# Turning four or six key tiles of the larger query groups by VectorE and DMA instead of TensorE, in a transformer block on one Trainium2 core

## The chip, the core and the metric

The kernel runs on one core of a Trainium2 chip (trn2). The metric is the time of one execution on the device in microseconds (us), the median of several runs. TensorE (PE) multiplies matrices, and PEld is its weight load; VectorE (DVE), ScalarE (ACT) and GpSimd (POOL) work beside it, and SyncE (SP) issues DMAs, each of which is carried out by the core's 16 DMA engines. Each engine runs its own list of instructions in order and waits only on semaphores.

## What is computed

One block with attention and a routed feed-forward network, in float32, on 2048 tokens of 128 features. The attention part, which takes most of the time, has 16 heads of 64 and is causal:

```python
qkv = jnp.einsum('bse,ehd->bshd', x, w_qkv)
q, k, v = jnp.split(qkv, 3, axis=-1)
logits = jnp.einsum('bqhd,bkhd->bhqk', q, k) / jnp.sqrt(jnp.float32(q.shape[-1]))
logits = jnp.where(mask, logits, neg)                      # causal
probs = jax.nn.softmax(logits, axis=-1)
out = jnp.einsum('bshd,hde->bse', jnp.einsum('bhqk,bkhd->bqhd', probs, v), w_out)
```

Ahead of it stands a layer norm with a scale and a shift, behind it a gated residual, a second layer norm, and a feed-forward network in which each token goes through one of 8 experts.

## The kernel before

The heads are taken in 8 pairs (`PAIRS`), the queries in 8 groups of 256 (`GROUPS`). A group g of a pair sees 2g+2 tiles of 128 keys (`tiles_of`), 72 tiles for all groups of a pair. Per pair and group the work is this:

- score (L803): for each of four rows r (two halves of 128 queries for each of two heads), TensorE makes the scores in pieces of up to 512 keys, each in one bank of a ring of four in PSUM.
- top (L1172, L1175, L1179): VectorE copies each piece into `probs`, which has one buffer for even and one for odd groups, and takes the row's maximum.
- exp (L1021): ScalarE makes the exponentials of a row in place, with their sum.
- turn (L814): the second product needs keys on the partitions, so TensorE transposes the 4 blocks of 128x128 of a key tile into one of three PSUM banks (`TURN_BANKS`). The last tile of a group has only 2 blocks.
- take (L1029 on ScalarE, L1197 on VectorE): one of the two copies the bank to one of 16 slots of `pT` (`PT_SLOTS`).
- pv (L832): TensorE multiplies the slot with the values, two heads in two halves of the array, and adds to `ps_o`. The tiles are taken in order, so those of a group must all be done before those of the next.
- sum, put, get, norm, out, add: the inverse sums are turned on VectorE (L1188, L1190), sent through DRAM by SyncE (put: 4 DMAs of L606; get: 2 DMAs of L617, which wait for the put to land), multiplied in (L1214), and the output projection follows (L845).
- proj, hi, lo: queries, keys and values of the next pair (L782, L786, L1007, L1151, L1155), placed between.

Each engine's order is computed ahead of time by the class `Plan`, from assumed durations of every step (`took`), conditions (`ready`) and a rule of choice (`choose_pe`, `choose`); `PV_BATCH`, `SCORE_LEAD`, `SCORE_TILES`, `TAKE_ACT` and `TAKE_DVE` are its constants. SyncE's order (`transfers`) is sorted by the same assumed times; 20 DMAs of zeros to DRAM (blank, L635) are put in it too. After the last score SyncE loads the expert weights (L640, L641, L645), the last into the buffer of `probs`. Then come the sorting of the tokens and the experts.

## Time and profile before

| | us |
|---|---|
| median of 3 runs | 987.63 (987.43 to 989.5) |
| the profiled execution | 984.52 |
| its span, first to last instruction | 982.7 |
| TensorE busy | 952.1 (97%) |
| VectorE busy | 708.8 (72%) |
| ScalarE busy | 675.3 (69%) |
| GpSimd busy | 110.2 (11%) |
| all DMA queues, share of 16 engines | 11.7% |

The engines overlap, so their busy times don't add up. A name such as L814 is a line of the kernel, and `ps<-ident,probs` are the tiles that an instruction writes and reads. One float32 matmul instruction of L832, L782 or L845 stands as two records in the trace, one of L803 or L814 as one. The duration of a matmul record holds the way through the array, so that the price of one in a row is the time from start to start.

### The profile page before, as it was taken

How to read it: one execution, taken by the hardware profiler on the slowest of the kernel's cores; microseconds unless marked ns; L12 is line 12 of the kernel's file. 1: busy time of each engine (PE TensorE's matmuls, PEld its weight loads, DVE VectorE, ACT ScalarE, POOL GpSimd, SP SyncE). 2: the span in 40 equal slices, each digit the busy share in tenths (PEclk: the TensorE clock that was granted, in tenths of full speed). 3: DMA queues.
4: the chain of work that ended last, by engine and by line, in shares of the span. 5: the costliest groups of instructions: out<-in, count | busy, mean ns of one | idle time of the engine just before them, and what ended most of it. 6: DMA issues, size and time to landing. Idle time of an engine off the chain costs nothing.

```text
span 982.7 us, 19699 instructions
## 1 busy us (share of the span) xinstructions
PE 952.1 (97%) x6851; PEld 747.2 (76%) x6851; DVE 708.8 (72%) x2362; ACT 675.3 (69%) x1245; POOL 110.2 (11%) x125
## 2 busy tenths in 40 slices
PE   3999999999999999999999999999999999999797
PEld 2677777777777777777777777777777777878797
DVE  5788648875788658784887758774887578986554
ACT  2887667666777658675876768666776677764475
POOL 0200001000100010000100010000100010202144
PEclk9999999999999999999999999999999999999899
DMA  3001100120011100110011000210010000005220
GB/s 81 10 14 50 26 21 15 31 51 20 11 36 25 29 18 21 50 26 20 15 32 34 23 23 12 51 26 20 14 31 18 12 8 11 27 14 176 64 64 26
DMA packets 56002, 30.78 MB, mean 31 GB/s; under 512 B 12455, under 2 KB 53203, under 8 KB 55906
## 3 DMA queue, kind: packets, MB, share of 16 engines
q1 hardware_dynamic: 54658, 27.41, 10.5%
q0 software_dynamic: 1248, 2.13, 0.7%
q8 instruction: 55, 0.90, 0.4%
q14 instruction: 41, 0.34, 0.1%
HBM read 18.21 MB, written 11.77 MB: 31 GB/s over the span
## 4 chain that ended last, share of the span: by engine, by line
PE 95%; DVE 2%; ACT 1%; DMA 1%; SPq 0%; issue 0%; POOLq 0%; POOL 0%; DVEq 0%; ACTq 0%
PE ps L803 27%; PE ps L832 25%; PE ps L814 25%; PE ps L782 6%; PE ps L786 3%; PE ps L845 3%; PE ps L956 2%; PE ps L967 2%; PE ps L931 0%; DMA probs<-in_L_wmod_dram 0%; DVE accT L1108 0%; PE ps L885 0%; PE ps L928 0%; DVE stats L1091 0%; PE ps L947 0%
## 5 line engine op out<-in xcount | busy, mean ns | idle before, releaser
L1021 ACT ACTIVATE probs<-probs,neg_max 128x128 f32<-128x128 f32 (+15 forms) x256 | 308.9, 1209 | 98.1 <-DVE neg_max L1179 96.4
L803 PE MATMUL ps<-k_both,q_both 128*128 128x512 f32 (+2 forms) x1280 | 360.2, 397 | 2.0 <-DVE k_both L1155 1.3
L814 PE MATMUL ps<-ident,probs 128*128 128x128 f32 x2176 | 297.7, 273 | 0.2
L1029 ACT COPY pT<-ps 128x512 f32<-128x512 f32 (+1 forms) x428 | 227.2, 564 | 87.6 <-PE ps L814 81.3
L814 PEld LDWEIGHTS ps<-ident,probs 128*128 128x128 f32 x2176 | 255.1, 141 | 42.3 <-issue 10.1
L1172 DVE TENSOR_SCALAR_CACHE_REDUCE probs<-ps 128x512 f32<-128x512 f32 (+1 forms) x384 | 247.0, 665 | 10.8 <-PE ps L803 8.7
L832 PE MATMUL ps<-pT,v_sb 128*64 128x256 f32 (+1 forms) x2304 | 250.0, 370 | 0.0
L803 PEld LDWEIGHTS ps<-k_both,q_both 128*128 128x128 f32 x1280 | 207.8, 190 | 50.5 <-issue 29.0
L832 PEld LDWEIGHTS ps<-pT,v_sb 128*64 128x64 f32 x2304 | 157.4, 137 | 80.5 <-issue 9.2
L707 POOL CAST k_both<-k_both 64x1024 fp32r<-64x1024 f32 x64 | 66.4, 1038 | 751.0 <-DVE k_both L1155 749.0
L1175 DVE CUSTOM_DVE_ANT_0 probs<-ps,causal 128x256 f32<-128x256 f32 (+3 forms) x256 | 130.5, 510 | 2.1 <-PE ps L803 1.2
L1197 DVE COPY pT<-ps 128x512 f32<-128x512 f32 (+1 forms) x148 | 96.9, 660 | 41.9 <-PE ps L814 40.5
L1151 DVE SCALAR_TENSOR_TENSOR q_both<-ps,q_both 64x512 fp32r<-64x512 f32 x64 | 44.1, 688 | 88.0 <-ACT q_both L1007 87.0
L782 PE MATMUL ps<-hT,w_pair 128*128 128x512 f32 x128 | 63.4, 609 | 0.9 <-ACT hT L993 0.9
L1014 ACT COPY v_sb<-ps 128x512 f32<-128x512 f32 x32 | 18.8, 586 | 58.8 <-PE ps L786 58.4
L1214 DVE TENSOR_TENSOR oT<-ps,rinv_b 128x512 f32<-128x512 f32 (+1 forms) x33 | 22.3, 675 | 40.4 <-PE ps L832 40.2
L1021 ACT ACTIVATION_READ_ACCUMULATOR probs<-probs,neg_max 128x1 f32 x256 | 49.5, 193 | 0.0
L1179 DVE TENSOR_REDUCE neg_max<-row_max 128x1 f32<-128x1 f32 (+3 forms) x256 | 39.8, 155 | 9.0
L1155 DVE TENSOR_TENSOR k_both<-ps,k_both 64x512 fp32r<-64x512 f32 x64 | 44.0, 687 | 1.4 <-ACT k_both L1007 0.2
L786 PEld LDWEIGHTS ps<-w_pair,hT 128*128 128x128 f32 x256 | 33.2, 196 | 12.9 <-issue 12.1
L1007 ACT ACTIVATE q_both<-ps 64x512 fp32r<-64x512 f32 x64 | 37.8, 590 | 5.5 <-PE ps L782 4.6
L1007 ACT ACTIVATE k_both<-ps 64x512 fp32r<-64x512 f32 x64 | 37.8, 590 | 1.5 <-PE ps L782 0.5
(142 smaller groups left out, 569.8 us busy)
## 6 DMA issues: line engine op xcount, KB each, us to landing
x_sorted<-blank SPq DMA_DIRECT2D x19, 458.5 KB, 5.3
rinv_b<-spread_rows SPq DMA_DIRECT2D x128, 64.0 KB, 2.6
spread_rows<-rinv_rows SPq DMA_DIRECT2D x256, 0.5 KB
probs<-in_L_ffn_W_dram SPq DMA_DIRECT2D x1, 2048.0 KB, 11.1
w_pair<-in_L_attn_w_qkv_dram SPq DMA_DIRECT2D x24, 64.0 KB, 2.2
hT<-x_sorted SPq DMA_DIRECT2D x23, 65.5 KB, 1.8
x_sb<-in_L_attn_x_dram SPq DMA_DIRECT2D x4, 256.0 KB, 5.1
wo_pair<-in_L_attn_w_out_dram SPq DMA_DIRECT2D x8, 64.0 KB, 1.8
```

Of the source, the lines that this page charges most:

```text
L707: nc.gpsimd.tensor_copy(k_split[h][own_half(1 - h), :, cols], k_split[h][own_half(h), :, cols]).then_inc(k_doubled[c], 1)
L782: pe.matmul(ps_ring[:, s.bank, :], w_pair[:, p % 2, j, :], hT[:, c * BANK:(c + 1) * BANK], start=True, stop=True).then_inc(bank_full[s.ban ...
L786: m = pe.matmul(ps_ring[:, s.bank, P * t:P * t + P], hT[:, (TPC * c + t) * P:(TPC * c + t + 1) * P], w_pair[:, p % 2, 2, :], start=True, s ...
L803: m = pe.matmul(ps_ring[:, s.bank, 0:w], q_split[r % 2][:, q0:q0 + P], k_split[r % 2][:, part, k0:k0 + w], start=(part == 0), stop=(part = ...
L814: m = pe.transpose(ps_turn[:, n % TURN_BANKS, P * r:P * r + P], probs[:, g % 2, r, j * P:j * P + P], ident[:])
L832: m = pe.matmul(ps_o[D * h:D * h + D, o_half + P * u0:o_half + QG], v_sb[:, j, D * h:D * h + D], turned[:, u0:2, h, :], start=(j == 0), st ...
L1007: m = act.mul(dst[own_half(h), c * BANK:(c + 1) * BANK], ps_ring[own_half(h), bank, :], Q_SCALE if j == 0 else 1.0)
L1021: act.activation(row, row, ACT.Exp, bias=neg_max[:, g, r:r + 1], accum_out=row_sum[:, g, r:r + 1]).then_inc(exp_done, 1)
L1029: act.copy(pT[:, n % PT_SLOTS, lo:BANK], ps_turn[:, n % TURN_BANKS, lo:BANK]).then_inc(turn_taken[n % TURN_BANKS], 1)
L1172: dve.tensor_scalar(row, ps_ring[:, bank, 0:w], 1.0, LOWEST, ALU.mult, ALU.max, accum_out=highest).then_inc(bank_free[bank], 1)
L1175: dve.tensor_tensor_reduce(row, ps_ring[:, bank, 0:w], causal[:, BANK - w:], 1.0, LOWEST, ALU.add, ALU.max, highest).then_inc(bank_free[ba ...
L1197: dve.tensor_copy(pT[:, n % PT_SLOTS, lo:BANK], ps_turn[:, n % TURN_BANKS, lo:BANK]).then_inc(turn_taken[n % TURN_BANKS], 1)
```

## The change

For the groups 4 to 7 the first key tiles (4 of group 4, 6 of each of the groups 5, 6 and 7, together 22 of the 72 tiles of a pair) are no longer turned by TensorE. Instead:

- shuffle, VectorE: one instruction for each row r transposes the 32x32 blocks of these tiles from `probs` into `staged`. It waits for the row's exponentials, and the first of a group also for the previous group's DMAs to have landed (`moved`).
- move, SyncE: 16 DMAs a group, one for each pair of a source quarter a and a target quarter b of the partitions. Each takes 32 partitions by 4 or 6 tiles by 512 B from `staged` to `turned_far`, so that the blocks come to lie transposed as a whole. They wait for the group's four shuffles and for the previous group's products with `turned_far`.
- pv: the products of a group start with the tiles that TensorE turned and end with the moved ones, read from `turned_far`; the first of those waits for all 16 DMAs of the group.

`staged` and `turned_far` have one buffer each. To make room, `pT` goes from 16 to 8 slots, and the even buffer of `probs` is shortened. The first score pieces of the group after next now also wait for the shuffles that read the same buffer. The constants of the plan change, so that the order of all engines is another one.

```diff
-PT_SLOTS = 16
-PV_BATCH = 15
-SCORE_LEAD = 1.6
-SCORE_TILES = 24.0
-TAKE_ACT = -1500.0
-TAKE_DVE = 0.0
+PT_SLOTS = 8
+STAGED = 6
+FAR = {4: 4, 5: 6, 6: 6, 7: 6}
+ISSUE = 430.0
+LAND = 4000.0
+PV_BATCH = 8
+SCORE_LEAD = 1.4
+SCORE_TILES = 18.0
+TAKE_ACT = 0.0
+TAKE_DVE = 2500.0
...
+def pv_order(g):
+
+    return list(range(far(g), tiles_of(g))) + list(range(far(g)))
...
-        turns = [(p, g, j) for p, g in groups for j in range(tiles_of(g))]
+        turns = [(p, g, j) for p, g in groups for j in range(far(g), tiles_of(g))]
+        pvs = [(p, g, j) for p, g in groups for j in pv_order(g)]
+        self.moves = [(p, g) for p, g in groups if far(g)]
...
+    def move_at(self, m):
+
+        if m not in self.moved:
+            p, g = self.moves[m]
+            begin = max(self.at("shuffle", p, g, r) for r in range(4))
+            if m:
+                q, f = self.moves[m - 1]
+                begin = max(begin, self.at("pv", q, f, far(f) - 1), self.move_at(m - 1)[0] + 16 * ISSUE)
+            if begin >= NEVER:
+                return NEVER, NEVER
+            self.moved[m] = begin + HOP, begin + HOP + 16 * ISSUE + LAND
+        return self.moved[m]
...
+                if s.kind == "move":
+                    g, a = s.key[1], s.key[2]
+                    m = plan.move_no[p, g]
+                    sp.wait_ge(shuffled, 4 * m + 4)
+                    if m:
+
+                        q, f = plan.moves[m - 1]
+                        sp.wait_ge(pv_done, plan.order[q, f, far(f) - 1] + 1)
+                    for b in range(P // SQUARE):
+                        sp.dma_start(turned_far[b * SQUARE:(b + 1) * SQUARE, 0:far(g), a, :],
+                                     staged[a * SQUARE:(a + 1) * SQUARE, 0:far(g), b, :]).then_inc(moved, 16)
+                elif s.kind == "w1":
...
+                elif s.kind == "w2":
...
+                    if j < far(g):
+                        if j == 0:
+                            pe.wait_ge(moved, 256 * plan.move_no[p, g] + 256)
+                        of_head = turned_far[:, j, :, :].rearrange("p a (u h i) -> p h u a i", u=2, h=2)
...
+                    if past and far(past[1]) and c == 0:
+
+                        dve.wait_ge(shuffled, 4 * plan.move_no[past] + r + 1)
...
+                elif s.kind == "shuffle":
+
+                    r, m = s.key[2], plan.move_no[p, g]
+                    dve.wait_ge(exp_done, 4 * (p * GROUPS + g) + r + 1)
+                    if m and r == 0:
+                        dve.wait_ge(moved, 256 * m)
+                    dve.transpose(staged[:, 0:far(g), :, r * SQUARE:(r + 1) * SQUARE],
+                                  probs[g % 2][:, r, 0:far(g) * P].rearrange("p (j b i) -> p j b i", j=far(g), i=SQUARE)
+                                  ).then_inc(shuffled, 1)
```

The line numbers of the changed kernel differ; its steps keep their order in the text. L874 is its score, L885 its turn, L910 its pv, L923 its out, L667 its move, L686 its put, L697 its get, L715 its blank, L1254, L1257 and L1261 its top, L1269 its shuffle and L1288 its take on VectorE.

TensorE, fourth pair, the end of group 5's turns and its products. Before:

```order
L814 MATMUL ps<-ident,probs 128x128 x6
L832 MATMUL ps<-pT,v_sb 64x256 x2
L832 MATMUL ps<-pT,v_sb 64x128 x2
L832 MATMUL ps<-pT,v_sb 64x256 x22
L832 MATMUL ps<-pT,v_sb 64x128 x2
L803 MATMUL ps<-k_both,q_both 128x512 x2
L803 MATMUL ps<-k_both,q_both 128x384 x2
L803 MATMUL ps<-k_both,q_both 128x512 x2
L845 MATMUL ps<-oT,wo_pair 128x512
```

The same place in the changed kernel:

```order
L885 MATMUL ps<-ident,probs 128x128 x2
L874 MATMUL ps<-k_both,q_both 128x512 x2
L874 MATMUL ps<-k_both,q_both 128x384 x2
L874 MATMUL ps<-k_both,q_both 128x512 x2
L910 MATMUL ps<-pT,v_sb 64x256 x10
L910 MATMUL ps<-pT,v_sb 64x128 x2
L910 MATMUL ps<-turned_far,v_sb 64x256 x12
L885 MATMUL ps<-ident,probs 128x128 x4
L874 MATMUL ps<-k_both,q_both 128x512 x2
L885 MATMUL ps<-ident,probs 128x128 x4
L874 MATMUL ps<-k_both,q_both 128x512 x2
L923 MATMUL ps<-oT,wo_pair 128x512
```

Twelve of group 5's products now read `turned_far` and stand behind those of the tiles that TensorE turned, and the projection of the output moves behind them.

SyncE, fourth pair, groups 3 to 6. Before:

```order
L606 DMA spread_rows<-rinv_rows 4x32 x4
L617 DMA rinv_b<-spread_rows 64x2x128 x2
L606 DMA spread_rows<-rinv_rows 4x32 x4
L617 DMA rinv_b<-spread_rows 64x2x128 x2
L635 DMA x_sorted<-blank 128x7x131
L606 DMA spread_rows<-rinv_rows 4x32 x4
L617 DMA rinv_b<-spread_rows 64x2x128 x2
L635 DMA x_sorted<-blank 128x7x131
```

The changed kernel, groups 4 to 7 of the same pair and the start of the next:

```order
L686 DMA spread_rows<-rinv_rows 4x32 x4
L667 DMA turned_far<-staged 32x4x128 x8
L697 DMA rinv_b<-spread_rows 64x2x128 x2
L715 DMA x_sorted<-blank 128x7x131
L667 DMA turned_far<-staged 32x4x128 x8
L686 DMA spread_rows<-rinv_rows 4x32 x4
L697 DMA rinv_b<-spread_rows 64x2x128 x2
L715 DMA x_sorted<-blank 128x7x131
L667 DMA turned_far<-staged 32x6x128 x16
L686 DMA spread_rows<-rinv_rows 4x32 x4
L697 DMA rinv_b<-spread_rows 64x2x128 x2
L715 DMA x_sorted<-blank 128x7x131
```

After these rows come 16 moves of group 6, the put of group 7, and group 7's moves in pieces of 4, 8 and 4, with group 7's get and the next pair's first put between the pieces. In the last pair the load of the third weight tensor (L680) stands before the last 4 moves of group 6, and the other two (L672, L673) before all 16 of group 7.

VectorE, fourth pair, the end of group 5. Before:

```order
L1151 SCALAR_TENSOR_TENSOR q_both<-ps,q_both 64x512 x2
L1188 RECIPROCAL rinv<-row_sum 128x4
L1190 STREAM_TRANSPOSE rinv_rows<-rinv 128x32
L1197 COPY pT<-ps 128x512
L1172 TENSOR_SCALAR probs,row_max<-ps 128x512
L1197 COPY pT<-ps 128x256
L1172 TENSOR_SCALAR probs,row_max<-ps 128x384
```

The same place in the changed kernel:

```order
L1229 SCALAR_TENSOR_TENSOR q_both<-ps,q_both 64x512 x2
L1279 RECIPROCAL rinv<-row_sum 128x4
L1281 STREAM_TRANSPOSE rinv_rows<-rinv 128x32
L1269 STREAM_TRANSPOSE staged<-probs 128x24x32 x4
L1316 SCALAR_TENSOR_TENSOR accT<-ps,gate_a,accT 128x512
L1257 ISA probs,row_max<-ps,causal 128x256
```

The four shuffles of group 5 stand in one run behind its sums, and the copies of turned tiles have left this place.

## Rows read from the trace of the kernel before

**Rows 1.** page, parts 1 and 2: busy engines; granted clock

```profile
PE 952.1 (97%) x6851; PEld 747.2 (76%) x6851; DVE 708.8 (72%) x2362; ACT 675.3 (69%) x1245; POOL 110.2 (11%) x125
...
PEclk9999999999999999999999999999999999999899
```

**Rows 2.** busy us (records) by stretch: PE, PEld, DVE, ACT, POOL, clock, DMA

```profile
266.00:287.47 21.47, 21.47 (x137) 17.18 (x137) 19.39 (x66) 17.83 (x32) 2.08 (x2) 1.00 0.05 14
179.20:287.47 108.27, 108.24 (x779) 83.62 (x780) 79.71 (x254) 76.96 (x136) 8.30 (x8) 1.00 0.10 26
```

**Rows 3.** the chain that ended last: shares by line; two of its pieces

```profile
by line: PE ps L803 27.0%; PE ps L832 24.9%; PE ps L814 24.7%; PE ps L782 5.5%; PE ps L786 3.2%; PE ps L845 2.9%; PE ps L956 2.3%; PE ps L967 2.1%; PE ps L931 0.5%; DMA probs<-in_L_wmod_dram 0.5%; DVE accT L1108 0.4%; PE ps L885 0.4%; PE ps
...
179.20 4.04 PE ps L832 x40
...
287.47 4.04 PE ps L832 x40
```

**Rows 4.** timeline of TensorE: start, duration, instruction, records

```profile
436.34 0.72 PE L803 MATMUL ps<-k_both,q_both 128*128 128x512 f32 x2
436.89 0.60 PE L814 MATMUL ps<-ident,probs 128*128 128x128 f32 x4
437.25 0.71 PE L803 MATMUL ps<-k_both,q_both 128*128 128x512 f32 x2
```

**Rows 5.** groups by form: copies out of PSUM, block transposes

```profile
L1029 ACT COPY pT<-ps 128x512 f32<-128x512 f32 x379 | 210.5, 587 | 78.2 <-PE ps L814 72.1 <-PE ps L832 2.4
...
L1197 DVE COPY pT<-ps 128x512 f32<-128x512 f32 x133 | 90.6, 686 | 17.7 <-PE ps L814 16.3 <-DVE onehot L1276 0.2
...
L1190 DVE STREAM_TRANSPOSE rinv_rows<-rinv 128x32 f32<-128x32 f32 x64 | 13.5, 212 | 2.2
...
L1197 DVE COPY pT<-ps 128x256 f32<-128x256 f32 x15 | 6.4, 424 | 24.2 <-PE ps L814 24.2
```

**Rows 6.** timeline of VectorE: start to start of a copy

```profile
440.37 0.69 DVE L1197 COPY pT<-ps 128x512 f32<-128x512 f32 x1
440.97 0.68 DVE L1172 TENSOR_SCALAR_CACHE_REDUCE probs<-ps 128x512 f32<-128x512 f32 x1
```

**Rows 7.** timeline of SyncE: DMA issues

```profile
453.06 1.26 SPq L606 DMA_DIRECT2D spread_rows<-rinv_rows  x4
455.20 1.23 SPq L617 DMA_DIRECT2D rinv_b<-spread_rows  x2
456.48 1.62 SPq L579 DMA_DIRECT2D w_pair<-in_L_attn_w_qkv_dram  x3
```

**Rows 8.** the loads of x: ns of one issue, min, median, max

```profile
L586 SPq DMA_DIRECT2D x_sb<-in_L_attn_x_dram x4: 434/480/507, 0.8 to 3.4; - x4
```

**Rows 9.** page, part 6: KB each, median us to landing

```profile
x_sorted<-blank SPq DMA_DIRECT2D x19, 458.5 KB, 5.3
rinv_b<-spread_rows SPq DMA_DIRECT2D x128, 64.0 KB, 2.6
...
w_pair<-in_L_attn_w_qkv_dram SPq DMA_DIRECT2D x24, 64.0 KB, 2.2
```

**Rows 10.** the 5.3 us of one blank DMA; DMA share before last

```profile
398.80:404.10 5.30, 5.30 (x34) 3.95 (x31) 4.21 (x13) 2.30 (x4) 0.00 (x0) 1.00 0.43 113
```

**Rows 11.** the last score of a group 4 on TensorE

```profile
498.91 0.48 PE L803 MATMUL ps<-k_both,q_both 128*128 128x256 f32 x2
```

**Rows 12.** ScalarE's last exponential of that group

```profile
501.71 1.37 ACT L1021 ACTIVATE probs<-probs,neg_max 128x1280 f32<-128x1280 f32 x1
```

**Rows 13.** timeline of SyncE: the expert weights

```profile
893.84 0.78 SPq L640 DMA_DIRECT2D w_rows<-in_L_ffn_W_dram  x1
894.67 6.49 SPq L641 DMA_DIRECT2D experts<-in_L_ffn_b_dram  x1
901.20 1.90 SPq L645 DMA_DIRECT2D probs<-in_L_ffn_W_dram  x1
```

**Rows 14.** that stretch: DMA share

```profile
898.00:911.00 13.00, 12.86 (x113) 9.73 (x110) 6.03 (x25) 4.22 (x9) 4.33 (x5) 1.00 1.01 343
```

More of the change, by code:

```diff
@@ L53, in tiles_of, with far @@
     return 2 * g + 2
+def far(g):
+    return FAR.get(g, 0)
+def pv_order(g):
+    return list(range(far(g), tiles_of(g))) + list(range(far(g)))
 def chunks(g):
@@ L103, in __init__ @@
         ends = [(PAIRS - 1, i) for i in range(len(parts_of(PAIRS - 1)))]
-        keys = dict(score=scores, turn=turns, pv=turns, out=norms,
+        keys = dict(score=scores, turn=turns, pv=pvs, shuffle=shuffles, out=norms,
                     proj=[(p, c, j) for p, c in parts for j in range(3)], back=ends,
@@ L113, in __init__ @@
         self.number = {key: i for i, key in enumerate(turns)}
+        self.order = {key: i for i, key in enumerate(pvs)}
+        self.move_no = {key: i for i, key in enumerate(self.moves)}
         self.total = {kind: len(of) for kind, of in keys.items()}
@@ L119, in __init__ @@
         self.taken = {}
+        self.moved = {}
         self.mode = ""
@@ L144 @@
                  act=("hi", "value", "take", "exp", "mod2", "wtake"),
-                 dve=("norm", "sum", "lo", "add", "resid", "top", "take", "smalls", "fresh", "pick", "slots", "ends"))
+                 dve=("norm", "sum", "lo", "shuffle", "add", "resid", "top", "take", "smalls", "fresh", "pick", "slots", "ends"))
     FIRST = dict(act=("hi", "value"), dve=("sum", "norm", "lo"))
@@ L166, in ready @@
             free = 0.0
-            if key[2] == 0 and p + g and min(groups_of(*self.part_of(p, g))) == g:
+            if key[2] == pv_order(g)[0] and p + g and min(groups_of(*self.part_of(p, g))) == g:
                 free = at("norm", *self.part_of(*group_before(p, g)))
-            return max(at("take", *key), at("value", p, key[2] // 4), free)
+            return max(self.turned_at(key), at("value", p, key[2] // 4), free)
+        if kind == "shuffle":
+            m = self.move_no[p, g]
+            return max(at("exp", *key), self.move_at(m - 1)[1] if m else 0.0)
         if kind == "out":
@@ L183, in ready @@
             if past and k0 < tiles_of(past[1]) * P:
-                behind = at("turn", past[0], past[1], min((k0 + w) // P, tiles_of(past[1])) - 1)
+                behind = at("shuffle", past[0], past[1], key[2]) if far(past[1]) else 0.0
+                over = min((k0 + w) // P, tiles_of(past[1])) - 1
+                if over >= far(past[1]):
+                    behind = max(behind, at("turn", past[0], past[1], over))
             return max(at("score", *key), behind)
@@ L220, in get_from, with turned_at @@
         return max(self.at("sum", p, g) + PUT, free)
+    def move_at(self, m):
[9 more added lines that the diff above has]
+        return self.moved[m]
+    def turned_at(self, key):
+        p, g, j = key
+        return self.move_at(self.move_no[p, g])[1] if j < far(g) else self.at("take", *key)
     def part_of(self, p, g):
@@ L241, in transfers @@
         self.blanks = [(i, min(i + BLANK_ROWS, rows // P)) for i in range(0, rows // P, BLANK_ROWS)]
+        for m, (p, g) in enumerate(self.moves):
+            for a in range(4):
+                steps.append((self.move_at(m)[0] + 4 * ISSUE * a, "move", (p, g, a)))
+        p, g = PAIRS - 1, GROUPS - 1
+        steps.append((self.at("score", p, g, 3, chunks(g) - 1), "w1", (p,)))
+        steps.append((max(self.at("turn", p, g - 1, tiles_of(g - 1) - 1),
+                          self.at("shuffle", p, g - 1, 3) if far(g - 1) else 0.0) + HOP, "w2", (p,)))
         quiet = [(p, g) for p in range(PAIRS - 1) for g in range(GROUPS - 4, GROUPS - 1)]
@@ L276, in took @@
                         "rank": 700.0, "total": 400.0}[kind] + switch
+        if kind == "shuffle":
+            return far(key[1]) * P / 0.96 + 100.0
         if kind == "top":
@@ L331, in choose_pe @@
         score_at = place("score", lambda k: (k[2] * chunks(k[1]) + k[3]) / (4.0 * chunks(k[1])))
-        turn_at = place("turn", lambda k: k[2] / float(tiles_of(k[1])))
+        turn_at = place("turn", lambda k: (k[2] - far(k[1])) / float(tiles_of(k[1]) - far(k[1])))
         waiting = 0
         for key in self.ahead["pv"]:
-            if self.at("take", *key) > now:
+            if self.turned_at(key) > now:
                 break
@@ L1026, in _ @@
                     if n >= PT_SLOTS:
-                        act.wait_ge(pv_done, n - PT_SLOTS + 1)
+                        act.wait_ge(pv_done, plan.order[plan.turns[n - PT_SLOTS]] + 1)
                     lo = 0 if j <= 2 * g else QG
@@ L1194, in _ @@
                     if n >= PT_SLOTS:
-                        dve.wait_ge(pv_done, n - PT_SLOTS + 1)
+                        dve.wait_ge(pv_done, plan.order[plan.turns[n - PT_SLOTS]] + 1)
                     lo = 0 if j <= 2 * g else QG
```

66 lines of the change are left out of this document (39 added, 27 removed).

## Prediction

> **What bounds the kernel now.** First the page's busy shares and its clock row: TensorE is busy for 952.1 of 982.7 us, at full granted clock in nearly every slice [rows 1]. Then stretches: one pair in the middle, 179.20 to 287.47, takes 108.27 us, and TensorE is busy for 108.24 of them, VectorE for 79.71, ScalarE for 76.96 [rows 2]; the product of each pair's group 4 starts 108.27 us after that of the pair before [rows 3]. So in the eight pairs nothing but TensorE's own list sets the time. Then the chain by line: the scores (L803) hold 27.0%, the products (L832) 24.9%, the turns (L814) 24.7% [rows 3]. What leaves TensorE there shortens the kernel, as long as nothing else becomes late.
>
> **TensorE's gain.** The turns' share is 24.7% of 982.7 = 242.7 us [rows 3]. A pair has 64 key tiles of 4 blocks and 8 last ones of 2, the 8 pairs 2176 blocks: 0.1115 us each. The change removes 22 of 72 tiles of a pair, 4 blocks each: 88 blocks, 9.81 us a pair, 704 blocks and **78.5 us** in all. In the same way one record of L832 costs 0.106 us (72 x 8 tiles of 4 records), so a tile of products 0.42; a query or key projection of 512 columns 0.84 (L782, 128 records), an output projection 0.86 (L845, 66 records). A score piece of 512 keys and a turned tile together take 0.91 us (436.34 to 437.25) [rows 4], so the piece is 0.46; I take 0.35 and 0.24 for pieces of 384 and 256.
>
> **VectorE and ScalarE.** By the order of the two kernels VectorE loses 82 copies of 512 columns and 8 of 256, 59.6 us by their durations; ScalarE loses 94 of 512 and gains 8 small ones, some 52 us [rows 5]. VectorE gains 96 shuffles of 768 elements a partition and 32 of 512. Such a size isn't in the trace. The nearest rows are the 32-element block transpose, 212 ns, and the copies from PSUM, 424 ns for 256 and 686 for 512 columns, so 1.02 ns a column behind a start of 162 [rows 5]. One column per 1.02 ns gives 195 for 32 columns, two steps per column 227; 212 lies between. Start to start a 512 copy takes 0.60 us [rows 6]. I take one step per column, 0.88 us for a shuffle of 768 and 0.62 for 512; the other end is 1.7 and 1.15. The sum for VectorE is 96 x 0.88 + 32 x 0.62 = 104 us against 60 removed: about 5.5 us more a pair, 85 of some 100. The Trainium skill (Vector Engine (DVE) Microarchitecture Reference, section 3.8) says that the transposing front end sustains one element per cycle and lane; by that my value stands, but no row here has a long one.
>
> **The path of the moved tiles.** The turn was on TensorE's own list; the moved tiles come by VectorE, SyncE and the DMA engines, and TensorE stands still if they are late, since nothing of its list can pass the waiting product. Price of one move on SyncE: the nearest in form is the load of x, rows of 512 B in four runs, 0.434 to 0.507 us, median 0.480 [rows 8]. In a row, puts take 1.26/4 = 0.32, loads of w_pair 1.62/3 = 0.54, gets 1.23/2 = 0.62 [rows 7]. I take 0.50 for one move, with ends 0.32 and 0.62 by issue alone. Data: a blank DMA, 128 x 7 = 896 packets of 524 B, filled 0.43 of 5.3 us on 16 engines [rows 10], 0.041 us per packet and engine. A move of six tiles is 192 packets, 12 per engine, 0.49 us: just within the issue. Landing: 2.2 to 2.6 us after the start of an issue for 64 KB [rows 9]; I take 2.2.
>
> From the landing of one group's tiles to that of the next: four shuffles 3.6 us (the first waits for that landing), 15 x 0.50 = 7.5 to the last issue, 2.2 to its landing, in all **13.3 us**. The group's put and get (1.3 + 0.9 wait + 1.2, and a blank 0.6) run beside the shuffles for groups 5 and 6. Against it stands what TensorE has to do between two groups' first moved products, by the order of the changed kernel at the prices above:
> - group 4 to 5: 12 pieces of 512, 2 of 384, 4 of 256, 22 blocks, 8 and a half tiles of products, one out: 14.5 us. No stall, 1.2 to spare.
> - 5 to 6: 10 and 1 pieces, 30 blocks, 12 and a half tiles of products, out and proj: 15.7. No stall, 2.4 to spare.
> - 6 to 7: 2, 2 and 4 pieces, 44 blocks, 14 and a half tiles: 14.1. Here SyncE also does group 7's get and the next pair's first put (1.2 + 1.3) between the moves: 15.8. **Stall 1.7.**
> - group 4 has no group ahead of it. From its last score to its last exponential the trace shows 499.2 to 503.1, 3.9 us [rows 11, 12]; then sum, one shuffle and put 1.7, 8 moves 4.0, get and blank 1.8, 7 moves 3.5, landing 2.2: 17.1. TensorE has 16.7 in between: **stall 0.4.**
>
> So 2.1 us a pair. Next is density. In the last stretch of a pair, 21.47 us, VectorE is busy for 19.39 already [rows 2]. Some 22 blocks leave it there, 2.5 us; VectorE gains group 7's four shuffles, 3.5, and loses about three copies of 0.6: 21.1 of work against 19.0 of TensorE's. The scores run up to 1.4 groups ahead and take part of it up; I count half, **1.0 a pair** (0 to 3). With only 8 slots the products come in more batches, 74 runs against 68, at some 0.15 each: 0.9 us in all.
>
> **The end of the last pair.** There SyncE's weight loads come ahead of moves. Before, they fill the DMA engines completely for 13 us at 343 GB/s (share 1.01) [rows 14], and the second issue held SyncE for 6.49 us, so that it came free 7.3 us after the first [rows 13]. In the changed order all 16 moves of group 7 stand behind these two: 7.3 + put 1.3 + 4 moves 2.0 + get 1.2 + 11 moves 5.5 + 2.2 = 19.5 from the last score, where TensorE has 15.4: 4.1 us. Group 6's last four stand behind a load of 2.1 MB (6.1 us at that rate), of which the 2.4 to spare are covered: 3.7. Together **7.8 us** (0 to 16).
>
> **Sum.** 78.5 - 8 x 3.1 - 0.9 - 7.8 = 45.0. The profiled execution took 984.52 us, 1.8 more than its span; 939.5 is what I expect of it. The median of the runs is 3.1 above the profiled one, so the forecast is **942.6 us**.
>
> **Rivals.**
> 1. The moves are fully hidden. An issue of 0.45 (the shortest load of x and a gap of 0.02) takes 0.75 off each path: group 4 is free, group 7 stalls 0.95, and if VectorE's dense stretch is taken up and the end costs 3, 67 us are saved: 921. For it: the DMA engines are only 10% busy [rows 2]; against it: VectorE is close to full.
> 2. The gain is mostly eaten, but not lost. An issue of 0.62, as the gets take: 1.8 us more per path, stalls 2.2 + 0.6 + 0 + 3.5 = 6.3, with density 7.3 a pair: 8 x 2.5 - 8.7 = 11 us saved, 976.
> 3. **Slower**: the moves are bound by data, since each reads 32 partitions and writes 32. From 0.65 us a move the stalls of a pair (3 x 2.28 + 0.9 = 7.7, with density and the end's share 9.8) equal the gain; at twice the packet time, 0.98 for six tiles and 0.65 for four, they are 2.7 + 6.0 + 4.8 + 8.9 = 22.4 a pair, and the kernel would take about 1105. No row has a DMA on so few partitions with so many packets, so neither end is excluded. The Trainium skill (SBUF — State Buffer, section on the DMA port swizzle) says that DMA bandwidth depends on how many of 16 SBUF ports the partitions reach, and by its table 32 neighbouring ones reach 8; by that rule the packets take up to twice as long and this case is the one, by the issue rows it isn't unless those packets lose more than a third.
> 4. Slower: shuffles take two steps per column, 1.7 us. The paths grow by 3.3 (group 4: 0.6): stalls 1.0 + 2.1 + 0.9 + 5.0 = 9.0, density 4: 13 a pair against 9.8, so 1022. For it: the 212 ns row; against it: it is as near to the other value.
> 5. The products with `turned_far` read runs of 32 columns. If that cost them double, 176 tiles x 0.42 = 75 us are lost, and the time doesn't change. No row shows such a read.
>
> **How the numbers follow.** Forecast (928 to 965) 0.52; rival 1 0.16; rival 2 (965 to 985.6) 0.13; no change within 0.2%, about what a measurement can tell, 0.04, with rival 5 in it; rival 3 0.10; rival 4 0.05. So faster 0.81, same 0.04, slower 0.15. Below 915 I leave 0.03 and above 985 the slower cases, so the range is 915 to 985.
>
> **What would show it.** TensorE: 1472 blocks of turns at the same 0.11 us; idle time in front of the first product with `turned_far`, put down to a DMA, 0 to 2 us, most in group 7, and longer at the end of the last pair. VectorE: shuffles of 0.9 to 1.0 us; 1.7 means rival 4. SyncE: 512 issues of 0.45 to 0.55; DMA share near 1 while they run and a landing far over 2.6 us after the last issue mean rival 3. Products with `turned_far` over 0.106 us a record mean rival 5. The forecast is wrong if VectorE, which waits for landed tiles in front of the next tops, holds up scores, so that TensorE waits for banks more than for moves.

## The result

The changed kernel takes 1032.53 us (median of 4 runs, 1032.12 to 1034.67) where the kernel before takes 988.08 beside it: a ratio of 1.045, with a 95% interval of 1.043 to 1.047. It is slower by 4.5%, where I had forecast a gain of 4.6%. The profiled execution of the changed kernel spans 1030.6 us, 47.9 more than the profiled one before. That one took 984.52 us, 3.6 less than the 988.08 here, so some 3.6 of the 47.9 are a difference between executions of the same kernel.

First the page of the changed kernel, its busy engines, its clock row and its chain by line (to be held against [rows 1] and [rows 3]).

```profile
span 1030.6 us, 18821 instructions
...
PE 919.4 (89%) x6147; PEld 681.8 (66%) x6147; DVE 758.8 (74%) x2400; ACT 626.7 (61%) x1159; POOL 110.2 (11%) x125
```

```profile
by line: SPq L667 24.1%; PE ps L910 11.5%; DMA turned_far<-staged 7.2%; PE ps L874 6.4%; PE ps L885 6.4%; issue 5.9%; DVE staged L1269 5.5%; PE ps L853 4.1%; DVE probs L1254 3.9%; PE ps L857 2.8%; PE ps L1034 2.3%; PE ps L1045 2.0%; DVE pro
```

TensorE did get its 704 blocks less, but its busy time fell by 33 us only, and it now stands idle for 111.2 us where it did for 30.6. In the chain, the largest single line is no longer one of TensorE's: SyncE's issue of the moves (L667) holds 24.1%.

Next the waits for the moves, of TensorE (PE), and the wait of VectorE (DVE) for the products that stand behind them (us in total, times, longest), and the moves' own row (duration of one issue in ns: min, median, max).

```profile
DVE oT L1305 <- PE ps L910: 63.1, 16, 8.7
...
PE ps L910 <- DMA turned_far<-staged: 58.7, 26, 11.1
```

```profile
L667 SPq DMA_DIRECT2D turned_far<-staged x512: 585/611/1881, 73.1 to 948.9; - x171
```

The fourth pair shows the path from landing to landing. First SyncE and then TensorE: start, duration, instruction, records, and in brackets the idle time ahead of it.

```profile
428.63 0.60 SPq L715 DMA_DIRECT2D x_sorted<-blank  x1
429.98 10.68 SPq L667 DMA_DIRECT2D turned_far<-staged  x16
441.22 1.26 SPq L686 DMA_DIRECT2D spread_rows<-rinv_rows  x4
...
445.98 10.60 SPq L667 DMA_DIRECT2D turned_far<-staged  x16
...
462.21 3.33 SPq L667 DMA_DIRECT2D turned_far<-staged  x4
465.64 1.27 SPq L697 DMA_DIRECT2D rinv_b<-spread_rows  x2
467.01 5.26 SPq L667 DMA_DIRECT2D turned_far<-staged  x8
472.32 1.51 SPq L686 DMA_DIRECT2D spread_rows<-rinv_rows  x4
473.93 2.56 SPq L667 DMA_DIRECT2D turned_far<-staged  x4
```

```profile
422.72 2.60 PE L910 MATMUL ps<-pT,v_sb 128*64 128x256 f32 x24 [1.26 <-DVE oT L1305]
426.43 1.95 PE L910 MATMUL ps<-turned_far,v_sb 128*64 128x256 f32 x16 [1.11 <-DMA turned_far<-staged]
...
442.43 2.81 PE L910 MATMUL ps<-turned_far,v_sb 128*64 128x256 f32 x24 [0.16 <-DMA turned_far<-staged]
...
458.63 2.76 PE L910 MATMUL ps<-turned_far,v_sb 128*64 128x256 f32 x24
...
478.27 4.38 PE L910 MATMUL ps<-turned_far,v_sb 128*64 128x256 f32 x24 [4.52 <-DMA turned_far<-staged]
```

```profile
426.39 3.56 DVE L1269 STREAM_TRANSPOSE staged<-probs 128x768 f32<-128x768 f32 x4 [1.84 <-DMA turned_far<-staged]
```

```profile
440.05 2.25 DMA turned_far<-staged
```

The last row is of the chain: from the start of the last issue to the landing. So the path is 3.56 for four shuffles, 10.07 from 429.98 to the last issue at 440.05, and 2.25 to land: from 426.39 to the next product of moved tiles at 442.43 it is 16.0 us, where I had 13.3. Of the 2.7 that are missing, 15 x 0.165 = 2.5 are the price of an issue. In front of group 7, with a get and a put between the moves, it is 19.6 (458.63 to 478.27), and TensorE is idle for 4.52 of them.

The stall has a second price. Below are stretches of that place: us, busy time of each engine, then the granted clock, the DMA engines' share and GB/s.

```profile
473.80:478.30 4.50, 0.03 (x2) 0.06 (x3) 1.02 (x5) 1.18 (x3) 0.00 (x0) 0.97 0.41 96
478.30:480.00 1.70, 1.70 (x9) 1.05 (x10) 0.00 (x0) 0.00 (x0) 0.00 (x0) 0.50 0.21 62
480.00:483.00 3.00, 3.00 (x21) 1.94 (x18) 0.32 (x1) 0.00 (x0) 0.00 (x0) 0.75 0.09 27
483.00:486.00 3.00, 3.00 (x18) 2.04 (x17) 0.52 (x2) 1.92 (x4) 0.00 (x0) 1.00 0.38 91
```

After 4.5 us without work TensorE was granted 0.50, its 1.2 GHz level, at once, and 0.75 on average over the 3 us behind; it was at 2.4 GHz again only after 483. The mean granted clock of the whole run is 0.965, before 0.993. The products with moved tiles, which stand right behind the stalls, carry most of it.

```profile
L910 PE MATMUL ps<-turned_far,v_sb 128*64 128x256 f32 x704 | 104.1, 454 | 58.7 <-DMA turned_far<-staged 58.7
```

A whole pair, from one group 7's moved products to the next pair's, now looks like this; before, it was 108.27 us with 108.24 busy [rows 2].

```profile
478.27:590.27 112.00, 102.62 (x689) 74.85 (x689) 85.53 (x256) 71.09 (x126) 8.29 (x8) 0.99 0.33 77
```

Of its 9.4 us of idle time the brackets below hold 8.7, and 7.5 of these are for moves.

```profile
532.57 2.60 PE L910 MATMUL ps<-pT,v_sb 128*64 128x256 f32 x24 [1.25 <-DVE oT L1305]
537.36 1.95 PE L910 MATMUL ps<-turned_far,v_sb 128*64 128x256 f32 x16 [2.19 <-DMA turned_far<-staged]
...
553.79 2.81 PE L910 MATMUL ps<-turned_far,v_sb 128*64 128x256 f32 x24 [0.59 <-DMA turned_far<-staged]
570.55 2.81 PE L910 MATMUL ps<-turned_far,v_sb 128*64 128x256 f32 x24 [0.41 <-DMA turned_far<-staged]
590.27 2.37 PE L910 MATMUL ps<-turned_far,v_sb 128*64 128x256 f32 x11 [4.28 <-DMA turned_far<-staged]
```

### The profile page after: what moved, and what is told of

Same layout as the page of the kernel before. It is cut to its first block, busy times and chain, and to the rows that moved or that the text cites. A ratio compares the mean times of both kernels' runs of the same rounds, so it can differ in the third digit from the quotient of the medians.

```text
span 1030.6 us, 18821 instructions
## 1 busy us (share of the span) xinstructions
PE 919.4 (89%) x6147; PEld 681.8 (66%) x6147; DVE 758.8 (74%) x2400; ACT 626.7 (61%) x1159; POOL 110.2 (11%) x125
## 4 chain that ended last, share of the span: by engine, by line
PE 38%; SPq 27%; DVE 17%; DMA 8%; issue 6%; ACT 3%; another core or an unknown queue 1%; POOLq 0%; POOL 0%; DVEq 0%; ACTq 0%
SPq L667 24%; PE ps L910 11%; DMA turned_far<-staged 7%; PE ps L874 6%; PE ps L885 6%; DVE staged L1269 6%; PE ps L853 4%; DVE probs L1254 4%; PE ps L857 3%; PE ps L1034 2%; PE ps L1045 2%; DVE probs L1257 2%; SPq L686 1%; SPq L697 1%; ACT probs L1099 1%
## 5 line engine op out<-in xcount | busy, mean ns | idle before, releaser
L1099 ACT ACTIVATE probs<-probs,neg_max 128x128 f32<-128x128 f32 (+15 forms) x256 | 308.9, 1207 | 150.2 <-DVE neg_max L1261 147.3
L874 PE MATMUL ps<-k_both,q_both 128*128 128x512 f32 (+2 forms) x1280 | 358.8, 397 | 9.0 <-DVE probs L1254 2.8
L1254 DVE TENSOR_SCALAR_CACHE_REDUCE probs<-ps 128x512 f32<-128x512 f32 (+1 forms) x384 | 245.5, 666 | 22.5 <-PE ps L885 10.8
L874 PEld LDWEIGHTS ps<-k_both,q_both 128*128 128x128 f32 x1280 | 203.7, 189 | 78.7 <-issue 28.7
L1107 ACT COPY pT<-ps 128x512 f32<-128x512 f32 (+1 forms) x342 | 178.1, 549 | 113.5 <-PE ps L885 104.8
L885 PE MATMUL ps<-ident,probs 128*128 128x128 f32 x1472 | 213.1, 274 | 1.4 <-ACT probs L1099 0.5
L885 PEld LDWEIGHTS ps<-ident,probs 128*128 128x128 f32 x1472 | 174.8, 141 | 42.3 <-issue 15.4
L910 PE MATMUL ps<-pT,v_sb 128*64 128x256 f32 (+1 forms) x1600 | 174.3, 366 | 9.9 <-DVE oT L1305 7.5
L910 PE MATMUL ps<-turned_far,v_sb 128*64 128x256 f32 x704 | 104.1, 454 | 58.7 <-DMA turned_far<-staged 58.7
L910 PEld LDWEIGHTS ps<-pT,v_sb 128*64 128x64 f32 x1600 | 108.2, 137 | 72.8 <-issue 12.4
L1257 DVE CUSTOM_DVE_ANT_0 probs<-ps,causal 128x256 f32<-128x256 f32 (+3 forms) x256 | 130.6, 510 | 26.4 <-PE ps L874 26.1
L1269 DVE STREAM_TRANSPOSE staged<-probs 128x768 f32<-128x768 f32 (+1 forms) x128 | 108.7, 886 | 41.9 <-DMA turned_far<-staged 40.5
L910 PEld LDWEIGHTS ps<-turned_far,v_sb 128*64 128x64 f32 x704 | 66.0, 163 | 88.2 <-issue 74.9
L1099 ACT ACTIVATION_READ_ACCUMULATOR probs<-probs,neg_max 128x1 f32 x256 | 49.0, 191 | 0.0
L1288 DVE COPY pT<-ps 128x512 f32<-128x512 f32 (+1 forms) x58 | 37.4, 656 | 12.2 <-PE ps L885 10.4
L1261 DVE TENSOR_REDUCE neg_max<-row_max 128x1 f32<-128x1 f32 (+3 forms) x256 | 39.8, 156 | 8.9
## 6 DMA issues: line engine op xcount, KB each, us to landing
x_sorted<-blank SPq DMA_DIRECT2D x19, 458.5 KB, 5.2
```

The costliest lines, as they stand in the source:

```text
L874: m = pe.matmul(ps_ring[:, s.bank, 0:w], q_split[r % 2][:, q0:q0 + P], k_split[r % 2][:, part, k0:k0 + w], start=(part == 0), stop=(part = ...
L885: m = pe.transpose(ps_turn[:, n % TURN_BANKS, P * r:P * r + P], probs[g % 2][:, r, j * P:j * P + P], ident[:])
L910: m = pe.matmul(ps_o[D * h:D * h + D, o_half + P * u0:o_half + QG], v_sb[:, j, D * h:D * h + D], of_head[:, h], start=(j == first), stop=( ...
L1099: act.activation(row, row, ACT.Exp, bias=neg_max[:, g, r:r + 1], accum_out=row_sum[:, g, r:r + 1]).then_inc(exp_done, 1)
L1107: act.copy(pT[:, n % PT_SLOTS, lo:BANK], ps_turn[:, n % TURN_BANKS, lo:BANK]).then_inc(turn_taken[n % TURN_BANKS], 1)
L1254: dve.tensor_scalar(row, ps_ring[:, bank, 0:w], 1.0, LOWEST, ALU.mult, ALU.max, accum_out=highest).then_inc(bank_free[bank], 1)
```

## The experiments

Three theories stood against each other. **A**: SyncE's issue of 16 DMAs, one behind the other, makes the path too long. **B**: the moves are bound by their data, because each reaches 32 partitions only (the mechanism of my rival 3). **C**: not the moves, but the other parts of the change cost the time: 8 slots of `pT` for 16, the planner's constants, VectorE. Ratios are to the kernel before on the same chip, with 95% intervals; the change itself stands at 1.045. The edits are shown shortened, and spans of runs on different chips can differ by some 0.4% (the kernel before took 984.1 to 989.0 us beside them).

### Half the bytes, the same 16 moves

```
-  turned_far[b*SQUARE:(b+1)*SQUARE, 0:far(g), a, :], staged[a*SQUARE:(a+1)*SQUARE, 0:far(g), b, :]
+  turned_far[b*SQUARE:(b+1)*SQUARE, 0:far(g)//2, a, :], staged[a*SQUARE:(a+1)*SQUARE, 0:far(g)//2, b, :]
```

> The changed kernel with all 16 moves of a group, but each carries only half of the tiles (2 of 4, 3 of 6), and the products read the first half twice: half of the bytes and packets, the same number of DMAs, the result is another one. Theory A, SyncE's issue sets the path: the issues stay at 0.61 to 0.67 us each in a row (0.665 in the changed kernel), only the last landing gets some 0.3 us shorter, so the time stays within 1018 to 1034. Theory B, the data of DMAs on 32 partitions sets it and the issue is held up by full queues: 16 moves take some 5.5 us instead of 10.6, the waits for moves vanish, time 940 to 965. Theory C, the moves aren't the cause but VectorE and the new order are: no change, but then the idle time before the products with turned_far is small, which it isn't (58.7 us); so A and C differ in the next run.

Measured: 1.028 (1.026 to 1.030), 1011.5 us, which is below theory A's 1018 to 1034 and far above theory B's 940 to 965. The issue row hardly moved with half the data, and 16 in a row took 11.17 us, no less than before.

```profile
L667 SPq DMA_DIRECT2D turned_far<-staged x512: 585/598/1890, 73.6 to 930.4; - x171
```

```profile
PE ps L910 <- DMA turned_far<-staged: 50.7, 24, 10.1
```

So the issue is a price of the DMA, not of its bytes, and B falls as the main cause: 50.7 of the 58.7 us of waiting stay. Some 1.7% do go with the bytes: the moves land 1.95 us after the last issue for 2.25, 8 us of waiting go, and the mean granted clock is 0.975 for 0.965.

### Eight moves of 64 partitions, the same bytes

```
-  for b in range(P // SQUARE):   turned_far[b*32:(b+1)*32, 0:far(g), a, :] <- staged[a*32:(a+1)*32, 0:far(g), b, :]
+  for b in range(2):             turned_far[b*64:(b+1)*64, 0:far(g), a, :] <- staged[(a//2)*64:(a//2+1)*64, 0:far(g), 2*(a%2)+b, :]
```

> The changed kernel with 8 moves of 64 partitions a group instead of 16 of 32: the same bytes and packets in half the DMAs; the blocks come to lie in the wrong quarters, so the result is another one. Theory A (issue): 8 x 0.67 = 5.4 us instead of 10.6, each group's path 5.3 us shorter, 10.7 against TensorE's 14 to 16 us of work, so no stalls in the middle: 78.5 us of turns minus about 1 us a pair and the end's, time 940 to 960. Theory B (data): the same 10.6 us for 8 moves, 1.3 us each, time 1025 to 1035. Theory C (VectorE, order): above 1000.

Measured: 0.976 (0.975 to 0.979). With half as many issues and all of the data, the loss of 4.5% is a gain of 2.4%, in a time (960.95 us) just above theory A's 940 to 960. This is the run that carries theory A: the path alone is changed. (The semaphore counts follow the number of DMAs.)

```profile
L667 SPq DMA_DIRECT2D turned_far<-staged x256: 590/638/1972, 73.4 to 874.9; - x128
```

```profile
PE ps L910 <- DMA turned_far<-staged: 20.0, 10, 10.0
```

```profile
412.80 8.13 SPq L667 DMA_DIRECT2D turned_far<-staged  x8
```

```profile
335.82 3.29 DMA turned_far<-staged
```

The path got shorter, but not by the 5.3 us that I had expected: a DMA alone issues in 0.59 to 0.64 us, but eight in a row take 1.02 each, and the landing has grown from 2.25 to 3.29. So it is 7.1 + 3.3 = 10.4 us behind the shuffles for 12.3 before, and in front of group 7, with its get and put, 16.5 (425.66 to 442.14) for 19.6. These 2 to 3 us a path are enough: half of the 20.0 us of waiting is one wait in the last pair.

What holds up eight in a row is the data. The first row below is of the change while moves alone are under way, the second of this run.

```profile
433.00:440.00 7.00, 7.00 (x42) 5.41 (x43) 6.89 (x26) 7.00 (x11) 0.00 (x0) 1.00 0.64 147
```

```profile
417.00:422.00 5.00, 5.00 (x29) 3.85 (x28) 4.57 (x15) 4.48 (x6) 0.00 (x0) 1.00 0.90 208
```

In the change the moves keep the DMA engines busy for 0.64 of the time, so that the data didn't hold up its issues; here it is 0.90. Both rows give the same price for a packet of 512 B and an engine: 0.64 x 16 x 512 B / 147 GB/s = 0.036 us on 32 partitions, and 0.035 on 64. By the rule of the Trainium skill (SBUF — State Buffer, section on the DMA port swizzle) I had let the packets take up to twice as long on 32 partitions. No run here settles that rule: by its table 64 neighbouring partitions reach the same 8 ports as 32, and no run moves from SBUF to SBUF on 128.

The run says more. TensorE has the same list in both kernels, so what differs is what the longer path cost. Here is a whole pair of this run, to be held against the one of 112.00 us above.

```profile
444.88:547.34 102.46, 99.90 (x691) 73.69 (x689) 85.40 (x256) 71.08 (x126) 8.30 (x8) 1.00 0.38 84
```

A pair should take 108.27 - 9.81 = 98.46 us of TensorE's work. Here it is busy for 99.90, 1.4 more, at full clock; in the change it was 102.62, another 2.7 more, and 9.4 us idle. Over the whole kernel TensorE is busy for 892.1 us here and 919.4 in the change.

### One contiguous run per partition

```
-  staged, turned_far: [P, STAGED, P // SQUARE, 4 * SQUARE]
+  staged, turned_far: [P, P // SQUARE, STAGED, 4 * SQUARE]
```

> The changed kernel with staged and turned_far laid out so that each move reads and writes one contiguous run per partition (32 runs of 3072 or 2048 B instead of 192 or 128 of 512 B): same DMAs, same bytes, same result. If the issue's cost comes from the shape (three dimensions or the number of runs), a move costs what the one with one run per partition costs, 0.36 us (wo_pair), 16 take some 6.2 us, and the time is 940 to 960. If the issue costs 0.6 us whatever the shape, it stays at 1025 to 1034. Theory B (data by bytes over few partitions): no change either, but with a DMA share near 1; by packets: down to 960.

Measured: 1.035 (1.033 to 1.037), 1018.7 us and so between the two expectations but near 1025, with 80578 packets for 154306. A move now reads and writes one run of 3072 B in each partition, and its issue falls only from 0.611 to 0.591 us (507 at the least), 16 in a row from 10.7 to 10.1 or 11.2. So neither the number of packets nor the shape is most of what costs, and a fifth of the loss is what could be had that way.

### The expert weights behind the moves

```
-  "w1": at(last score of the last pair);  "w2": behind the last shuffle of group 6
+  "w1": behind the last move of group 7;  "w2": behind the last move of group 6
```

> The changed kernel with the three expert weight loads of the last pair put behind the moves instead of between them, nothing else. In the changed kernel group 6's moved tiles of the last pair are waited for 11.1 us, and the loads stand ahead of them. If the loads' data in the queues hold up the moves: 8 to 12 us less, 1020 to 1025. If the wait there comes from elsewhere, or the weights are then late themselves by as much: 1030 to 1035.

Measured: 1.042 (1.040 to 1.044). TensorE's longest wait for moves falls from 11.1 us to 5.1, but by the ratio the kernel gains only 0.3%, some 3 us (the spans differ by 6.1), and it then waits 2.6 for the weights. The end of the last pair is a small part of the loss.

### No moves, but everything else of the change

```
-  FAR = {4: 4, 5: 6, 6: 6, 7: 6}
+  FAR = {}
```

> The changed kernel with no moved tiles at all: TensorE turns all 72 as before, but with the 8 slots, the constants and the shortened buffer of the change. If the moves alone are the cause of the loss (theory A), this is within 1.5% of the kernel before, since TensorE has its whole list back and no wait for DMAs: ratio 1.00 to 1.015. If the smaller buffer and the new constants cost much themselves (theory C), the ratio is above 1.03.

Measured: 1.020 (1.017 to 1.023). That is more than theory A allows for: what the change pays for its two buffers, before a tile is moved, costs 2%. Is it the slots or the constants? The next run takes the other constants back and leaves the 8 slots (and batches of 8, which they force).

```
-  SCORE_LEAD = 1.4, SCORE_TILES = 18.0, TAKE_ACT = 0.0, TAKE_DVE = 2500.0
+  SCORE_LEAD = 1.6, SCORE_TILES = 24.0, TAKE_ACT = -1500.0, TAKE_DVE = 0.0
```

> No tile is moved, pT has 8 slots as in the change and products come in batches of 8, but lead, tiles and the biases of the copies are those of the kernel before (1.6, 24, -1500, 0). no_far, with the constants of the change, took 1.020. If the 8 slots cost it (92 runs of products for 68, and VectorE and ScalarE waiting for slots): 1.010 to 1.020 again. If the constants did: 1.000 to 1.005.

Measured: 1.019 (1.017 to 1.021). It is the slots, then, or the batches of 8 that come with them. The page shows no new stall; TensorE's busy time has grown by 13.9 us over the 952.1 of [rows 1] with the same work.

```profile
PE 966.0 (97%) x6851; PEld 748.7 (75%) x6851; DVE 692.1 (69%) x2335; ACT 691.0 (69%) x1272; POOL 110.4 (11%) x125
```

The timeline has 93 runs of products where before has 68. A pair takes 109.75 us for 108.3, measured between the value projections of two pairs, which is 12 us in eight pairs. So theory C has a part of its own, some 17 us. Why the busy time grows is not shown: 25 more runs at the 0.15 us of the prediction would be 3.8.

### The planner told the true prices

```
-  ISSUE = 430.0;  LAND = 4000.0
+  ISSUE = 665.0;  LAND = 2300.0
```

> The changed kernel with the plan's assumed durations set to the measured ones: 0.665 us per move instead of 0.43, 2.3 us from the last issue to the landing instead of 4.0, so that the order of all engines allows for 12.9 us of moving a group instead of 10.9. If the loss is a wrong order (the moved products stand too early in TensorE's list), most of it comes back: ratio below 1.01. If it is the length of the path itself, which three groups in a row with one buffer each have to go through within TensorE's work of 14 to 16 us (16.0 measured), the stalls move but stay: ratio 1.02 to 1.045.

Measured: 1.057 (1.052 to 1.061), slower than the change and above both expectations. The wait for the moves is 59.3 us, as before. An order that knows how long the moves take did not help here. And with the constants of the fastest kernel below (batches of 6, lead 1.5, 22 tiles, biases -1500 and 1000) all four groups came out worst of all:

> All four moved groups (4: 4 tiles, 5, 6 and 7: 6 each) as in the change, but with the planner's constants of the kernel called best1 (a move priced at 665 ns, batches of 6 products, lead 1.5, 22 tiles, copies biased to ScalarE by 1500 ns and away from VectorE by 1000). Theory A (the path of 16 us between two landings, three of them back to back, sets the time whatever the order is): 4 to 5 us of stall per group stay at group 7 and about 2 at each of two others, so 1.03 to 1.05 times the kernel before. Theory C (the constants of the change put the work in a bad order, the moves themselves fit): 0.98 to 1.01.

Measured: 1.106 (1.103 to 1.108). Waits for the moves are 56.4 us again, but TensorE also waits 20.4 us for `k_both` of the next pair and 15.0 for exponentials. So the order costs or saves several per cent beside the moves; I had expected 1.03 to 1.05, or 0.98 to 1.01, and both theories missed it. What exactly in that order makes the projections late, I have not traced.

### Fewer and other groups

```
   without_g7:  FAR = {4: 4, 5: 6, 6: 6}, constants of the change
   g456_new:    FAR = {4: 4, 5: 6, 6: 6}, constants of best1
   best1:       FAR = {3: 4, 5: 6, 6: 6}, ISSUE 665, LAND 2300, PV_BATCH 6, SCORE_LEAD 1.5, SCORE_TILES 22, TAKE_ACT -1500, TAKE_DVE 1000
```

> The changed kernel, its plan's durations untouched, with tiles of groups 4, 5 and 6 moved, those of group 7 turned by TensorE again: 128 DMAs, 32 shuffles less, 192 blocks (21.4 us of TensorE) more. Group 7's path is the longest in the changed kernel (the stall before its moved products is 4.5 us in the middle pairs, and some 1.9 us of work at half clock follow). Theory A: 8 x (4.5 + 1.9) plus some 11 us at the end come back, 2.7 us a pair are paid for the turns: about 40 us less than the changed kernel, ratio 1.00 to 1.01. If the loss sits in VectorE or in all groups alike, the ratio is 1.03 or more.

> Only groups 4, 5 and 6 move tiles (4, 6 and 6), with the planner's constants of best1. It differs from without_g7 (1.018) by the constants alone, and from best1 (0.971) by its first moved group alone, group 4 for group 3. Theory A (moved groups that follow each other directly leave TensorE less work than the path takes): the stalls of 2 us in front of two of the three groups of a pair, 40 us in all in without_g7, stay; 1.00 to 1.02. Theory C (constants): they go, 0.965 to 0.98, as best1.

> Moved tiles in groups 3 (4 tiles), 5 and 6 (6 each), none in 4 and 7, with the plan's durations as measured (0.665 and 2.3 us) and its other constants chosen anew for that. 16 tiles a pair leave TensorE, 7.1 us a pair, 57 us in all. Between the groups 3 and 5 lie two groups of TensorE's work, only 5 to 6 follows directly, and the end of the last pair has no moves after the weight loads. Theory A: the paths (3.6 + 10.0 + 2.3 us) are covered except a us or two a pair: ratio 0.95 to 0.975, faster than the kernel before. If moves cost something that isn't on their path (VectorE's shuffles, contention), the ratio stays above 0.985.

Measured: 1.018 (1.015 to 1.021), 1.012 (1.010 to 1.014) and 0.971 (0.968 to 0.973). Without group 7's moves the kernel does 192 blocks more on TensorE (21 us of work) and is still 2.6% faster than the change: these moves lose more than they give, though 1.018 is above the 1.00 to 1.01 that I had expected. What is left are stalls of about 2 us in front of groups 4 and 6. (In without_g7 the waits for moves are 40.0 us, 10.9 of them one wait in the last pair.) The new constants alone give 0.5%. Then one edit, group 3 in place of group 4 at the same number of tiles, takes 4.1% off.

```profile
L910 PE MATMUL ps<-turned_far,v_sb 128*64 128x256 f32 x512 | 69.0, 422 | 40.0 <-DMA turned_far<-staged 40.0
```

```profile
PE ps L910 <- DMA turned_far<-staged: 15.5, 9, 5.2
PE ps L885 <- ACT probs L1099: 12.4, 6, 2.1
```

```profile
L910 PE MATMUL ps<-turned_far,v_sb 128*64 128x256 f32 x512 | 63.2, 396 | 8.4 <-DMA turned_far<-staged 8.3
```

The first of these fences is of without_g7, the second of g456_new, the third of best1. They don't bear theory A out as its expectation had it, though 1.012 lies in its range. The waits for moves were to stay at some 40 us in g456_new, and they fell to 15.5: the stalls in front of group 6 are gone but for one of 5.2 us in the last pair, and those of group 4 (0.7 to 2.0 us) remain. In their place came 12.4 us of waiting for exponentials (L1099), so that the time hardly moved. And from g456_new to best1, 33.7 us of span, only 7.2 are waits for moves; 12.4 are those waits for exponentials, 10.9 are busy time, and some 3 are other waits. With groups 3, 5 and 6 only 5 and 6 follow each other directly, and of the 8.3 us that are left 6.3 are one wait at the end, behind a load of weights. That this choice of groups is faster is shown; that it is so because of the moves' path is shown for a small part only.

### A version that beats both

best2 is best1 with both loads of expert weights behind the last move and the contiguous runs from above.

> best1 (0.971) with the expert weights loaded behind the last move and with each partition's tiles as one run in both buffers. In best1 TensorE waits 6.25 us for the last group's moves, behind a load of weights, and 2 us for all others together. Theory A: those 6 us go and an issue is 0.03 us shorter, 0.963 to 0.968. If the late weights are then waited for instead, 0.970 or more.

Measured: 947.15 us against 984.71 before on that chip, 0.962 (0.960 to 0.964).

```profile
PE 905.0 (96%) x6339; PEld 690.5 (73%) x6339; DVE 729.9 (77%) x2362; ACT 649.3 (69%) x1213; POOL 110.5 (12%) x125
...
L910 PE MATMUL ps<-turned_far,v_sb 128*64 128x256 f32 x512 | 60.8, 385 | 0.4 <-DMA turned_far<-staged 0.3
```

The moves are fully hidden (0.3 us of waiting), and the mean granted clock is 0.992. Its span is 944.5, 38.2 less than before. The 512 blocks that leave TensorE are worth 57.1 by my price of 0.1115, and 57.1 less the 17.4 that no_far_old's span shows for the slots (1000.1 - 982.7) is 39.7. So the two terms together give what this run shows, within 1.5 us; each by itself it doesn't show, since its other constants differ too.

## Why the prediction was wrong

**The step that failed** is the price of one move on SyncE: "I take 0.50 for one move, with ends 0.32 and 0.62 by issue alone". Alone it is 0.585 to 0.61, and in a row of 16 it is 10.6/16 = 0.665, above my upper end. I took it from the load of x, a DMA of 128 partitions from DRAM; no row had one from SBUF to SBUF on 32 partitions, and I set the end of the range at the dearest row I had, the gets. My own arithmetic had the rest: with 2.5 us more per path my stalls become 1.3, 0.1 and 4.2 for groups 5, 6 and 7 and 2.9 for group 4, together 8.5 us a pair for the 2.1 forecast. The pair above has 7.5 (0.6 + 0.4 + 4.3 + 2.2). Over eight pairs these are 51 us more, and the sum gives about 990, 6 us over the 984.52 before. The waits came out smaller than that: 5.0 to 7.5 us in each of the pairs between the first and the last, and 58.7 in the whole kernel where I had 24.6 (8 x 2.1 + 7.8), 34 more. That the length of the path is what decides is shown by eight_moves, where it alone is changed: 2 to 3 us less in each, and 38.7 us of waiting, 27.3 of busy time and 6.7 of other idle time are gone. I had written the break-even, "from 0.65 us a move", under rival 3, but tied it to the data: the threshold was right, the mechanism wrong (the issues take 0.665 while the DMA engines are 0.64 busy), and its chance of 0.10 was that of the mechanism, not of the threshold. Between 0.62 and 0.65 I had left out a case.

**What the sum did not have.** My sum ended 92.9 us below the profiled execution (939.5 for 1032.4), and the 34 of the waits for moves are the smaller part. Other idle time is 22 for the 8 that I gave to density, and 45 are busy time of TensorE, for which I had 0.9. The span grew by 47.9, and the two pages account for it: 78.5 of blocks taken away, 80.6 of idle time added (111.2 for 30.6; 58.7 waits for moves, 7.5 for `oT`), and 45.8 of busy time over the 873.6 that I should have seen (919.4). The 45.8 divide like this:
- TensorE at its lower clock behind each stall, which I had at nothing. In eight_moves, with the same list and most stalls gone, TensorE is busy for **27.3 us** less (1030.6 us at a mean granted clock of 0.965, 957.9 at 0.986). Most of it is in the 704 records of products with moved tiles: 104.1 us here, 85.3 there, and at best2's 60.8/512 they would be 83.6.
- 18.5 us stay when most stalls are gone. The 8 slots are a part: I had 0.9 us for 74 runs of products instead of 68, and in no_far_old they are **17.4 us**, of which 13.9 is busy time. A pair in the middle agrees, with 1.4 us of busy time over the sum in eight_moves and 1.5 more span in no_far_old. That run moves nothing, so its 13.9 need not be the size of this part in the change.
- Some 5 us are left. A record of a product with moved tiles, start to start, is 0.112 us (24 from 458.63 to 461.32), for the 0.106 of my sum: 4 us for 704. Part of that may be the start of a run. The rest stays open.

**Point by point.** TensorE's gain: the sum of best2 agrees with it. VectorE: 85 us a pair forecast, 85.53 measured. The shuffles: 3.56 for four, 0.89 each, for my 0.88; rival 4 is out. The landing: 2.25 for 2.2. By the Trainium skill (Vector Engine (DVE) Microarchitecture Reference, section 3.8) the front end takes one element per cycle and lane, and the trace agrees: 948 ns for 768 columns on average, where two steps would be 1.7 us. Rival 5 (products read runs of 32 columns at double cost): out, since the 24 records took 2.81 us at full clock, 0.117 each, start included. The price of a packet, 0.041 us: read wrongly, as the stretch of [rows 10] moved 113 GB/s x 5.3 us = 600 KB and not only the blank's 458.5; for the moves 0.036 is measured, and nothing of the forecast hung on it but the end of rival 3. The stall of group 7, 1.7 forecast: 3.8 to 4.6. The path there is 3.8 longer than mine, 2.5 by the price of an issue, 0.6 because a get, a put and their gaps took 3.1, the rest because moves in three pieces take 0.70 each; TensorE's own work took 1.0 more than my 14.1 and so covers some of it. Group 4: 0.4 forecast, 1.0 to 2.2 from the second pair on. Order of size among the groups: 7 was the largest as forecast, then 4, but 5 and 6, which I had without a stall, have 0.2 to 1.3 in most pairs. The end of the last pair: 7.8 forecast, one wait of 11.1 and 2.4 more behind it; late_weights shows that it decides little. Rival 3: the right number to watch, the wrong reason, and far from its 1105. What I named as what would make the forecast wrong, VectorE late with the scores, did not happen: TensorE waits 9.0 us in front of scores in all.

## What to carry to other kernels

Before a step leaves the bounding engine, lay the path that replaces it end to end and compare it with the work that engine has between two arrivals; with a margin of 1 us per path, the price of one DMA issue times its count decided here, and where no row has that form of DMA, take an upper end above the dearest row at hand and give the break-even a chance of its own. Count the DMAs before the bytes, and the bytes too once the engines come near full: half the DMAs were worth 6.9 points here, half the bytes 1.7. One moved group put elsewhere was worth 4.1%, of which waits for moves were a fifth, so look at every wait and not at the one that you had in mind. A stall of some us on TensorE costs more than itself, and buffers that are halved to make room have a price that can be run by itself, with the new step left out.
